# Attention with a fused projection: moving the row maxima of two query tiles within a slot

## The chip, the cores and the metric

One Trainium2 chip, one core. The time is device microseconds for one execution of the whole kernel, the median of several runs. Smaller is better.

## The reference

Sixteen images of 512 channels and 32 x 32 = 1024 positions go through an attention layer with 8 heads of 64 channels, an output projection with bias, a normalisation by the mean square over channels and a residual:

```python
qkv = jnp.einsum('bchw,oc->bohw', x, w_qkv)
q, k, v = jnp.split(qkv, 3, axis=1)
q = q.reshape(b, HEADS, HEAD_DIM, n) * SCALE        # HEAD_DIM 64, SCALE 64 ** -0.5
sim = jnp.einsum('bhdi,bhdj->bhij', q, k)
attn = jax.nn.softmax(sim, axis=-1)
out = jnp.einsum('bhij,bhdj->bhid', attn, v)
y = jnp.einsum('bchw,oc->bohw', out, w_out) + b_out[None, :, None, None]
mean_sq = jnp.mean(y * y, axis=1, keepdims=True)
y = y * jax.lax.rsqrt(mean_sq + SCALE) * rms_scale[None, :, None, None]
return y + x
```

## The kernel before

**Tiling.** A batch (image) is worked off in 8 slots; a slot is one pair of heads (slot // 2) and one half of 512 query positions (slot % 2). Within a slot there are 8 steps, one for each tile of 128 keys, and 16 places, t = 0 to 15. At every even place t TensorE computes the scores of step t / 2 for the two heads of the pair (`scores`, lines 707 and 716: two products per head, since every operand is kept as a high and a low part). ScalarE turns them into `probs` (L816), GpSimd adds the probs up in `prob_sum` (L1211, L1207), and TensorE multiplies them with the values (`values`, L729) into `pv`. The values of steps 0 to 3 of a slot run at place 9 of it, those of steps 4 to 7 at place 1 of the next slot, followed by `sums` (L648), which adds the partitions of `prob_sum`.

**What fills the odd places.** The work for later slots is put at odd places by `items_at`, which lists items and the PSUM bank of each (0 to 3 of the tile `aux`). Q, K0, K1 and V0 to V3 are projections (L549 for Q and K, L587 for V); O0 and O1 are the output projection (L616), R the mean of squares, T the transposed maxima (L601). The items M0 to M3 (called M00, M01 and so on, the second digit being the head) are products of one tile of 128 queries with all keys of the next slot; VectorE takes their row maxima (L1040), which stand in for the softmax maximum. One head's product fills two banks: M00 takes banks 0 and 1, M01 banks 2 and 3. In M1 and M3 the first head is counted in two pieces, M10 in bank 0 and N10 in bank 1: VectorE reduces bank 0 first (L1046), which frees it, then the rest (L1052); M11 is in banks 2 and 3. The maxima's matmuls have line 673 for tile 0 and line 692 for the others.

**What sets the order.** Every engine runs a program written out by hand, in order. An item that writes a bank first waits in `claim` until all earlier items in that bank have been read (`aux_free`); with `two=True` it waits for the bank beside it as well. VectorE handles at each place first the items of `items_at` in their order (maxima, k_l of the K items at L1033, and so on), then the reciprocals of the softmax sums (`invert_sums`, L1098, two halves, at INVERT_SUMS_AT), then `normalise` (L1105, at NORMALISE_AT), then its share of the normalisation of y (`invert`, L1092; `scale_y`, L1111, at SCALE_AT). ScalarE copies K to `k_hh` (L848), V to `v_sb` (L858), the sums to `inv_sum` (L879), and makes `o_hi` (L885, at OUTPUT_HIGH_AT); GpSimd makes `o_lo` (L357) in front of the addition of step 4 and adds the residual (`add_resid`, L1233) at the steps of RESIDUAL_AT in slots 1 and 2. The output product O0 stands at place 11 and needs `o_lo`.

Before, at place 1, TensorE runs: values of steps 4 and 5; M0; values of steps 6 and 7; sums; M1. At place 9 it runs the values of steps 0 to 3, M2 in front of the value number VALUES_FIRST[slot], and M3 at the end. Place 3 has K0 in slots 0, 2 and 4, a V item in slots 1, 3, 6 and 7, and nothing in slot 5; places 5 and 7 have the two halves of K1 in slots 0, 2 and 4, V items in others.

Of the kernel before, what the change touches and what calls it, by code (L numbers as in the profile page):

```python
# [17 lines left out]

SLOTS, STEPS, TILES = 8, 8, 4
PLACES = 2 * STEPS
SLOT_QUERIES = 2
RING = 6


INVERT_SUMS_AT = ((2, 2),) * 8
NORMALISE_AT = (2,) * 8
OUTPUT_HIGH_AT = (4, 8, 4, 4, 4, 6, 4, 4)
OUTPUT_LOW_AT = 4  # L30

REPEAT_K_AT = (8, 9)
# [2 lines left out]
SPLIT_MAXIMA = (1, 3)  # L35


VALUES_FIRST = (2, 1, 2, 1, 2, 1, 2, 1)


TURN_OF_MAXIMA = 7
# [12 lines left out]
SCALE_BY_GPSIMD = ((0,), (0, 1))  # L54
SCALE_BY_ACT_AT = ((0, 8), (1, 8))
SCALE_AT = ({1: (1, 1), 2: (1, 3), 3: (1, 4)}, {2: (2, 4), 3: (2, 10)})
RESIDUAL_AT = ((0, 1, 4, 4), (0, 1, 4, 5))


SPLIT_HIGH_AT = ((5, 0),) * 4 + ((6, 0),) * 4  # L60
# [11 lines left out]
def items_at(slot, t, first, last):  # L72

    following = not (last and slot == SLOTS - 1)
    projected = not (last and slot >= SLOTS - SLOT_QUERIES)
    preceding = not (first and slot == 0)
    out = []
    if t in (1, 9) and following:
        for it in (0, 1) if t == 1 else (2, 3):
            out.append((f"M{it}0", 0))  # L80
            if it in SPLIT_MAXIMA:
                out.append((f"N{it}0", 1))
            out.append((f"M{it}1", 2))
    if t == 3 and slot in (0, 2, 4):
        out.append(("K0", 0))
    elif t == 3 and (slot in (1, 3) or slot == 6 and projected or slot == 7 and following):
        out.append(({1: "V0", 3: "V2", 6: "V1", 7: "V2"}[slot], 0))
    if t == 5 and slot == 6 and projected:
        out.append(("K0", 1))
    if t == 7:  # L90
        if slot in (0, 2, 4):
            out.append(("K1", 1))
        elif slot in (1, 3):
            out.append((f"V{slot}", 1))
        elif slot == 5 and not last:
            out.append(("V0", 1))
        elif slot == 6 and projected:
            out.append(("K1", 2))
        elif slot == 7 and following:
            out.append(("V3", 1))  # L100
    if (slot, t) in MEAN_AT and not first:
        out.append(("R", 2))
    if t == (11 if following else LAST_OUTPUT_AT) and preceding:
        out.append(("O0", 0))
    if t == (13 if following else LAST_OUTPUT_AT) and preceding:
        out.append(("O1", 2))
    if t == 15:
        if following:
            out.append(("T", 2))
        if projected:  # L110
            out.append(("Q", 0))
    return out
# [33 lines left out]
def attention_kernel(nc, x, wqkv, wout, bias, scale, consts, out):  # L146
# [27 lines left out]
    with ctx:  # L174
# [330 lines left out]
        def _(pe):  # L505
            def claim(body, slot, name, two=False):

                k, n = body.at(slot, name)
                if body.plan is not pro or n > 0:
                    pe.wait_ge(aux_free[k], n)  # L510
                if two:
                    claim_beside(body, slot, name)
                return k

            def claim_beside(body, slot, name):
                other, n = beside_counts(body.plan, body.b, (slot, name))
                if body.plan is not pro and pro.end[other] or body.plan is pro and n > 0:
                    pe.wait_ge(aux_free[other], n)

            def wait_w(body, chunk, next_batch):  # L520
# [32 lines left out]
            def item(body, slot, name, turn=None, part=None):  # L553
# [19 lines left out]
                elif name[0] == "V":  # L573
                    chunk = VA if slot >= 5 else VB
                    if body.plan is not pro:
                        k = body.at(slot, name)[0] if part == 1 else claim(body, slot, name)
                    wait_w(body, chunk, slot >= 5)
                    w = w_ring[:, RING_OF[chunk]]
                    for i in range(2) if part is None else (part,):
                        jt = 2 * int(name[1]) + i  # L580
                        n = 0
# [152 lines left out]
            def one(body):  # L734
                for slot in range(SLOTS):
                    if body.first and slot == 0:
                        pe.wait_ge(q_repeated, 2)
                        pe.wait_ge(k_repeated, 4)
                    before = (body, SLOTS - 1, True) if slot == 0 else (body, slot - 1, False)
                    preceding = not (body.first and slot == 0)  # L740
                    for t in range(PLACES):
                        names = [name for name, _ in items_at(slot, t, body.first, body.last)]
                        if t % 2 == 0:
                            scores(body, slot, t // 2)
                        elif t == 1:
                            if preceding:
                                values(before[0], before[1], 4, before[2])
                                values(before[0], before[1], 5, before[2])
                            if "M00" in names:
                                maxima_of_tile(body, slot, 0)  # L750
                            if preceding:
                                values(before[0], before[1], 6, before[2])
                                values(before[0], before[1], 7, before[2])
                                sums(body, slot)
                            if "M10" in names:
                                maxima_of_tile(body, slot, 1)
                        elif t == 9:
                            for j in range(STEPS // 2):
                                if j == VALUES_FIRST[slot] and "M20" in names:
                                    maxima_of_tile(body, slot, 2)  # L760
                                if j == 2 and "O0" in names:
                                    item(body, slot, "O0")
                                    item(body, slot, "O1")
                                values(body, slot, j, False)
                            if "M30" in names:
                                maxima_of_tile(body, slot, 3)
                        else:
                            if t == 5:
                                for name, _ in items_at(slot, 7, body.first, body.last):
                                    if in_halves(slot, name):  # L770
                                        item(body, slot, name, part=0)
                            if t == 13 and body.last and slot == SLOTS - 1:
                                values(body, slot, 4, False)
                                values(body, slot, 5, False)
                                item(Body(epi, B - 1, False, True), 0, "R0")
                            for name in names:
                                if t == 7 and in_halves(slot, name):
                                    item(body, slot, name, part=1)
                                elif name == "Q":
                                    item(body, slot, "Q", (body, slot))  # L780
                                elif name != "T" or "Q" not in names:
                                    item(body, slot, name)
# [542 lines left out]
```

## Time and profile before

| | us |
|---|---|
| median of 3 runs | 3956.9 |
| lowest and highest | 3954.56, 3996.69 |
| the profiled execution's own time | 3978.09 |
| its span, first to last instruction | 3976.0 |
| TensorE busy | 3911.9 (98%) |
| VectorE busy | 2803.0 (70%) |
| ScalarE busy | 2313.7 (58%) |
| GpSimd busy | 2966.9 (75%) |
| mean granted TensorE clock | 0.994 of full speed |

Busy time is the time in which an engine had an instruction in work. For TensorE the ends of matmuls are modelled and neighbouring matmuls overlap, so distances between starts say more than durations. A row that groups several instructions gives the start of the first, the time that they covered, and their number.

### The profile page before, as it was taken

The page shows a single profiled execution, that of the slowest core. Times are in us where ns is not written, and L with a number is a line of the kernel's source. Part 1 is how long each engine was busy: PE and PEld are TensorE (multiplying, and loading weights), DVE is VectorE, ACT ScalarE, POOL GpSimd, SP SyncE. Part 2 cuts the span into 40 slices and gives each one's busy share as a digit, 9 for nine tenths or more (in the row PEclk, how much of TensorE's full clock was granted, in tenths as well). Part 3 has the DMA queues.
Part 4 walks back from the last instruction along what each step waited for, and adds up shares of the span by engine and source line. Part 5 has one row for each costly group of instructions (what it writes and reads, how often), then busy time and mean ns, then how long its engine had stood idle before and what let it go on. Part 6 is the DMA issues. An engine that isn't in the chain of part 4 may idle for free.

```text
span 3976.0 us, 53150 instructions
## 1 busy us (share of the span) xinstructions
PE 3911.9 (98%) x18630; PEld 2460.2 (62%) x18630; DVE 2803.0 (70%) x2899; ACT 2313.7 (58%) x4048; POOL 2966.9 (75%) x2332
## 2 busy tenths in 40 slices
PE   8999999999999999999999999999999999999997
PEld 5666666656666666665666666666665666666663
DVE  6667676676766767677686776767667676676775
ACT  4556565555655656565565665655556556565654
POOL 5678777776877778777787777877777777787776
PEclk9999999999999999999999999999999999999998
DMA  3111111111111201102011020111111111111100
GB/s 149 49 47 54 43 67 51 43 54 43 67 51 43 74 22 70 58 33 75 27 67 56 35 72 32 64 54 38 69 54 43 54 38 69 54 51 45 63 33 22
DMA packets 71847, 212.18 MB, mean 53 GB/s; under 512 B 8216, under 2 KB 9368, under 8 KB 58784
## 3 DMA queue, kind: packets, MB, share of 16 engines
q1 hardware_dynamic: 71584, 208.80, 14.7%
q8 instruction: 150, 2.46, 0.3%
q14 instruction: 113, 0.93, 0.1%
HBM read 168.92 MB, written 39.85 MB: 53 GB/s over the span
## 4 chain that ended last, share of the span: by engine, by line
PE 96%; DVE 1%; issue 1%; ACT 0%; DMA 0%; POOL 0%; SPq 0%; ACTq 0%; DVEq 0%; POOLq 0%
PE pv L729 24%; PE aux L549 17%; PE score L707 13%; PE score L716 12%; PE aux L587 9%; PE aux L616 9%; PE aux L692 7%; PE pv L648 3%; PE aux L673 2%; ACT probs L816 0%; DVE inv_sum L1098 0%; DVE k_l L1033 0%; PE aux L601 0%; DVE maxima L1040 0%; PE aux L626 0%
## 5 line engine op out<-in xcount | busy, mean ns | idle before, releaser
L1211 POOL TENSOR_TENSOR prob_sum<-prob_sum,probs 128x512 f32<-128x512 f32 x1536 | 1964.6, 1308 | 356.6 <-ACT probs L816 356.6
L816 ACT ACTIVATE probs<-score 128x512 f32<-128x512 f32 x2048 | 1111.0, 595 | 783.8 <-PE score L716 777.3
L1040 DVE TENSOR_REDUCE maxima<-aux 128x1 fp32r<-128x1024 f32 x768 | 914.0, 1218 | 416.1 <-PE aux L692 269.8
L729 PE MATMUL pv<-probs,v_sb 128*64 128x512 f32 x4096 | 998.1, 608 | 0.0
L707 PE MATMUL score<-q_hl,k_hh 128*128 128x512 f32 x2048 | 841.8, 411 | 9.1 <-ACT probs L816 9.1
L716 PE MATMUL score<-q_hm,k_l 72*128 72x512 f32 x2048 | 814.7, 398 | 0.5 <-DVE q_hm L1058 0.5
L549 PE MATMUL aux<-x_hi,w_ring 128*128 128x512 f32 x2048 | 654.6, 397 | 10.2 <-DMA scale_sb<-scale 9.3
L1207 POOL TENSOR_TENSOR prob_sum<-probs 128x512 f32<-128x512 f32 x256 | 325.1, 1292 | 393.7 <-ACT probs L816 391.6
L729 PEld LDWEIGHTS pv<-probs,v_sb 128*64 128x64 f32 x4096 | 249.6, 136 | 483.4 <-issue 475.6
L707 PEld LDWEIGHTS score<-q_hl,k_hh 128*128 128x128 f32 x2048 | 387.5, 189 | 179.4 <-issue 87.0
L549 PEld LDWEIGHTS aux<-x_hi,w_ring 128*128 128x128 f32 x2048 | 387.3, 189 | 97.6 <-DMA scale_sb<-scale 9.3
L1098 DVE RECIPROCAL inv_sum<-inv_sum 128x256 f32<-128x256 f32 x254 | 427.0, 1723 | 8.6 <-ACT inv_sum L879 5.7
L716 PEld LDWEIGHTS score<-q_hm,k_l 72*128 72x128 f32 x2048 | 388.3, 190 | 69.1 <-DVE q_hm L1058 1.1
L549 PE MATMUL aux<-x_lo,w_ring 128*128 128x512 f32 x1024 | 401.3, 392 | 0.0
L587 PE MATMUL aux<-w_ring,x_hi 128*128 128x256 f32 x1984 | 363.1, 282 | 0.0
L692 PEld LDWEIGHTS aux<-k_hh,q_hm 64*128 64x128 f32 x762 | 117.8, 186 | 345.9 <-issue 268.2
L587 PEld LDWEIGHTS aux<-w_ring,x_hi 128*128 128x128 f32 x1984 | 320.6, 191 | 17.3
L1058 DVE TENSOR_TENSOR q_hm<-aux,tile_mask 8x512 fp32r<-8x512 f32 x256 | 163.7, 676 | 223.2 <-PE aux L601 223.2
L1046 DVE TENSOR_REDUCE aux<-aux 128x1 f32<-128x513 f32 x256 | 179.3, 700 | 192.4 <-PE aux L692 189.6
L692 PE MATMUL aux<-k_hh,q_hm 64*128 64x512 f32 x762 | 291.8, 455 | 19.8 <-DVE k_l L1033 17.8
L1074 DVE TENSOR_TENSOR y_sb<-y_sb,aux 128x1024 f32<-128x1024 f32 x192 | 232.7, 1212 | 111.0 <-PE aux L616 110.3
L692 PE MATMUL aux<-k_hh,q_hl 64*128 64x512 f32 x762 | 291.9, 456 | 0.0
(114 smaller groups left out, 5123.6 us busy)
## 6 DMA issues: line engine op xcount, KB each, us to landing
w_ring<-w_split SPq DMA_DIRECT2D x93, 1024.0 KB, 4.8
stage<-x SPq DMA_DIRECT2D x252, 256.0 KB, 4.6
out<-stage SPq DMA_DIRECT2D x124, 256.0 KB, 2.0
w_split<-w_ring SPq DMA_DIRECT2D x3, 1024.0 KB, 12.3
w_split<-y_sb SPq DMA_DIRECT2D x3, 1024.0 KB, 3.8
y_sb<-wqkv SPq DMA_DIRECT2D x4, 512.0 KB, 8.5
probs<-wqkv SPq DMA_DIRECT2D x2, 512.0 KB, 7.2
probs<-wout SPq DMA_DIRECT2D x1, 1024.0 KB, 8.2
```

Source lines behind the costliest of these rows:

```text
L549: last = pe.matmul(out_ap, w[:, wp, k, cols], xp[:, k, xcols], start=(k == 0 and n == 0), stop=(k == KT - 1 and n == 2))
L587: last = pe.matmul(to[:, i * WCOLS:(i + 1) * WCOLS], xp[:, c, jt * P:(jt + 1) * P], w[:, wp, c, :], start=(n == 0), stop=(n == 3 * KT - 1))
L616: last = pe.matmul(bank(k + i), w[:, pair, m * P:(m + 1) * P], o[:], start=(n == 0), stop=(n == 2))
L692: last = pe.matmul(bank(k + h), q_hi_at(nhalf, e, h, it), k_hh[rows, npair % 2, e, h * HALF:(h + 1) * HALF], start=True, stop=True)
L707: pe.matmul(score[e][:], k_hh[:, pair % 2, e, keys], q_hl[:, half, e, :], start=True, stop=False)
L716: pe.matmul(score[e][:], k_l1[0:D + 2 * IT, pair % 2, e, keys], q_hm[0:D + 2 * IT, half, e, :], start=False, stop=True).then_inc(score_rea ...
L729: pe.matmul(pv[half][e * D:(e + 1) * D, :], v_sb[:, pair // 2, j, (pair % 2) * P + e * D:(pair % 2) * P + (e + 1) * D], probs[:, (b * SLOT ...
L816: act.activation(probs[:, step % RING, e, :], score[e][:], ACT.Exp, scale=SOFT).then_inc(prob_ready, 1)
L1040: dve.tensor_reduce(maxima[:, n:n + 1], bank(k, 2), AX_X, ALU.max).then_inc(aux_free[k], 1)
L1098: dve.reciprocal(inv_sum[:, cols], inv_sum[:, cols]).then_inc(inv_ready, 1)
L1207: pool.tensor_tensor(prob_sum[:, e, :], probs[:, (step - 1) % RING, e, :], probs[:, step % RING, e, :], ALU.add).then_inc(prob_added, 1)
L1211: pool.tensor_tensor(prob_sum[:, e, :], prob_sum[:, e, :], probs[:, step % RING, e, :], ALU.add).then_inc(prob_added, 1)
```

## The change

At place 1 TensorE computes all four values and the sums, then M0. M1 moves to place 3, behind the scores of step 1 and in front of the projection of that place; VectorE's list moves with it, since both go by `items_at`. VectorE inverts the sums and normalises the output at place 4 in place of 2, and ScalarE makes `o_hi` at place 8 in every slot. In slots 3 and 7 M2 stands in front of all values of place 9 (VALUES_FIRST 1 becomes 0), and the V item of place 7 goes to bank 3 in place of bank 1, with a claim on bank 2 too. The residual adds of the second half, in slot 2, move from steps 4 and 5 to 2 and 4. The banks of the maxima stay as they are.

```diff
-INVERT_SUMS_AT = ((2, 2),) * 8
-NORMALISE_AT = (2,) * 8
-OUTPUT_HIGH_AT = (4, 8, 4, 4, 4, 6, 4, 4)
+INVERT_SUMS_AT = ((4, 4),) * 8
+NORMALISE_AT = (4,) * 8
+OUTPUT_HIGH_AT = (8,) * 8
...
-VALUES_FIRST = (2, 1, 2, 1, 2, 1, 2, 1)
+VALUES_FIRST = (2, 1, 2, 0, 2, 1, 2, 0)
...
-RESIDUAL_AT = ((0, 1, 4, 4), (0, 1, 4, 5))
+RESIDUAL_AT = ((0, 1, 4, 4), (0, 1, 2, 4))
...
-    if t in (1, 9) and following:
-        for it in (0, 1) if t == 1 else (2, 3):
+    if t in (1, 3, 9) and following:
+        for it in {1: (0,), 3: (1,), 9: (2, 3)}[t]:
...
         elif slot in (1, 3):
-            out.append((f"V{slot}", 1))
+            out.append((f"V{slot}", 1 if slot == 1 else 3))
...
         elif slot == 7 and following:
-            out.append(("V3", 1))
+            out.append(("V3", 3))
...
-                        k = body.at(slot, name)[0] if part == 1 else claim(body, slot, name)
+                        k, _ = body.at(slot, name)
+                        if part != 1:
+
+                            claim(body, slot, name, two=k == 3)
...
                                 values(before[0], before[1], 5, before[2])
-                            if "M00" in names:
-                                maxima_of_tile(body, slot, 0)
-                            if preceding:
                                 values(before[0], before[1], 6, before[2])
                                 values(before[0], before[1], 7, before[2])
                                 sums(body, slot)
-                            if "M10" in names:
-                                maxima_of_tile(body, slot, 1)
+                            if "M00" in names:
+                                maxima_of_tile(body, slot, 0)
...
                         else:
+                            if "M10" in names:
+                                maxima_of_tile(body, slot, 1)
...
-                            for name in names:
+                            for name in [name for name in names if name[0] not in "MN"]:
```

## Rows read from the trace of the kernel before

**Rows 1.** The page: busy time by engine (its share of the span); the chain.

```profile
PE 3911.9 (98%) x18630; PEld 2460.2 (62%) x18630; DVE 2803.0 (70%) x2899; ACT 2313.7 (58%) x4048; POOL 2966.9 (75%) x2332
...
PE 96%; DVE 1%; issue 1%; ACT 0%; DMA 0%; POOL 0%; SPq 0%; ACTq 0%; DVEq 0%; POOLq 0%
```

**Rows 2.** Waits of TensorE: line, what it waited for, us in total, times, longest.

```profile
PE aux L692 <- DVE k_l L1033: 17.8, 3, 6.0
```

**Rows 3.** Timeline of TensorE, slot 2 into 3: start, us, what, number.

```profile
2061.53 0.40 PE L707 MATMUL score<-q_hl,k_hh 128*128 128x512 f32 x1
2061.77 0.39 PE L716 MATMUL score<-q_hm,k_l 72*128 72x512 f32 x1
2062.09 1.94 PE L729 MATMUL pv<-probs,v_sb 128*64 128x512 f32 x8
2063.96 0.49 PE L673 MATMUL aux<-k_hh,q_hm 64*128 64x512 f32 x1
...
2064.62 1.94 PE L729 MATMUL pv<-probs,v_sb 128*64 128x512 f32 x8
2066.38 1.03 PE L648 MATMUL pv<-prob_sum,ones_d 128*64 128x512 f32 x4
2067.34 0.49 PE L692 MATMUL aux<-k_hh,q_hm 64*128 64x512 f32 x1
...
2068.00 0.50 PE L707 MATMUL score<-q_hl,k_hh 128*128 128x512 f32 x1
2068.34 0.40 PE L716 MATMUL score<-q_hm,k_l 72*128 72x512 f32 x1
...
2069.05 0.62 PE L549 MATMUL aux<-x_hi,w_ring 128*128 128x512 f32 x2
...
2094.19 0.50 PE L673 MATMUL aux<-k_hh,q_hm 64*128 64x512 f32 x1
...
2096.62 1.03 PE L648 MATMUL pv<-prob_sum,ones_d 128*64 128x512 f32 x4
```

**Rows 4.** Timeline of VectorE: one row of slot 1, then slot 2.

```profile
2039.67 0.78 DVE L1111 SCALAR_TENSOR_TENSOR y_sb<-y_sb,scale_sb,rms_a 128x512 f32<-128x512 f32 x1
...
2064.72 2.36 DVE L1040 TENSOR_REDUCE maxima<-aux 128x1 fp32r<-128x1024 f32 x2 [0.39 <-PE aux L673]
2067.91 0.70 DVE L1046 TENSOR_REDUCE aux<-aux 128x1 f32<-128x513 f32 x1 [0.83 <-PE aux L692]
...
2069.25 1.21 DVE L1040 TENSOR_REDUCE maxima<-aux 128x1 fp32r<-128x1024 f32 x1
2070.38 3.35 DVE L1098 RECIPROCAL inv_sum<-inv_sum 128x256 f32<-128x256 f32 x2
2073.77 0.69 DVE L1105 TENSOR_TENSOR o_norm<-inv_sum,pv 128x512 f32<-128x512 f32 x1
...
2075.79 1.84 DVE L1111 SCALAR_TENSOR_TENSOR y_sb<-y_sb,scale_sb,rms_a 128x512 f32<-128x512 f32 x1
2077.66 1.39 DVE L1033 TENSOR_TENSOR k_l<-aux,k_hh 64x512 fp32r<-64x512 f32 x2
2079.87 2.36 DVE L1040 TENSOR_REDUCE maxima<-aux 128x1 fp32r<-128x1024 f32 x2 [0.82 <-PE aux L692]
```

**Rows 5.** Timeline of TensorE at place 9 of slot 2: M2.

```profile
2079.33 0.50 PE L692 MATMUL aux<-k_hh,q_hm 64*128 64x512 f32 x1
```

**Rows 6.** Timeline of TensorE's weight loads there: M3's second head.

```profile
2082.28 0.18 PEld L692 LDWEIGHTS aux<-k_hh,q_hm 64*128 64x128 f32 x1 [0.24 <-DVE maxima L1040]
```

**Rows 7.** Timeline of ScalarE, slot 2: copies of K0.

```profile
2071.98 1.21 ACT L848 ACTIVATE k_hh<-aux 64x512 fp32r<-64x512 f32 x2 [2.11 <-PE aux L549]
```

**Rows 8.** Timeline of VectorE and TensorE, slot 2 of the fourth batch.

```profile
843.81 7.97 DVE L1111 SCALAR_TENSOR_TENSOR y_sb<-y_sb,scale_sb,rms_a 128x512 f32<-128x512 f32 x1
...
853.35 0.76 PE L692 MATMUL aux<-k_hh,q_hm 64*128 64x512 f32 x1 [5.95 <-DVE k_l L1033]
```

**Rows 9.** Windows there: length, busy by engine (number), granted clock, DMA share, GB/s.

```profile
853.00:860.00 7.00, 6.65 (x20) 2.61 (x21) 3.57 (x5) 0.18 (x1) 0.12 (x1) 0.59 0.10 37
```

**Rows 10.** Timeline of GpSimd, the end of slot 2.

```profile
2089.12 5.02 POOL L1211 TENSOR_TENSOR prob_sum<-prob_sum,probs 128x512 f32<-128x512 f32 x4
```

More of the change, by code:

```diff
@@ L516, in claim_beside @@
                 other, n = beside_counts(body.plan, body.b, (slot, name))
-                if body.plan is not pro and pro.end[other] or body.plan is pro and n > 0:
+                if n > 0:
                     pe.wait_ge(aux_free[other], n)
```

## The prediction

> **What bounds the kernel.** I read the page first: TensorE is busy for 98% of the span, and the chain that ended last is TensorE for 96% [rows 1]. VectorE (70%) and GpSimd (75%) have room on average. So the time is the length of TensorE's stream, and an edit counts by what it adds to that stream: slower switching between kinds of matmul, or a wait. The waits say that there is hardly one: the largest entry is 17.8 us in three pieces [rows 2]. All three are one event: a VectorE scaling that took 7.97 us where its neighbour takes 1.84, after which TensorE stood 5.95 us [rows 8], and the granted clock of the next 7 us was 0.59, that is, a mixture of 2.4 and 1.2 GHz [rows 9]. One such event costs 5.95 + 0.41 x 7 = 8.8 us at most, three about 26 us. The profiled execution took 3978.1 us; without them it would be near 3952, next to the 3954.6 to 3956.9 of two of the three unprofiled runs. So I add my sum to the median, 3956.9 (on the profiled execution's own time it is the same sum on 3978.1).
>
> Next, the timeline of TensorE at place 1 of one slot [rows 3], slot 2, which stands for all 128. Its order is: values of steps 4 and 5 (1.87 us), M0 (0.66), values of 6 and 7 (1.76), sums (0.96), M1 (0.66), then the scores of step 1 (1.05), then the projection. The reader should see that nothing waits. Then VectorE over the same slot [rows 4]: it starts on M0 0.76 us after M0's first matmul and needs 2.36 us for its two reductions. They end at 2067.08, and M1, which writes the same banks, starts at 2067.34. M0's reductions are hidden under values and sums, with 0.26 us to spare. That cover is what the change takes away.
>
> **Moving M0 behind the sums and M1 behind the scores of step 1.** Let T be the start of M0. Before, M1 came at T + 3.38. Now only the scores of step 1 lie between: M0 0.66, scores 1.05, and a score-to-maxima switch that the trace of before does not have. Its bounds are 0 and 0.10 us, the latter the step from score to values (0.32 us from the last score matmul to the first value, where a score follows a score in 0.23 [rows 3]); I take 0.10. So M1 is next on TensorE at T + 1.8.
> The banks are not free then. M10 takes banks 0 and 1, which M00 held: its reduction ends at T + 0.76 + 1.23 = T + 2.0. M11 takes banks 2 and 3, which M01 held: T + 0.76 + 2.36 = T + 3.12. With 0.05 us for the semaphore M11 starts at T + 3.17. The 0.05 and the wait itself can be seen at place 9: M2 starts at 2079.33, its reductions end at 2079.87 + 2.36 = 2082.23, and the weights of M3's second head are loaded at 2082.28 [rows 5, 6]. There M3 comes 2.53 us behind M2 and still waits a little; M1 would now come 1.8 us behind M0.
> Then the projection (K0, V0, V2 or V1, by slot) claims bank 0, which M10 has to leave. VectorE can start M10's 0.70 us reduction only when both of M0's are done, so bank 0 is free at T + 3.12 + 0.70 + 0.05 = T + 3.87. Without waits the projection would start at T + 1.8 + 0.66 = T + 2.45. That is 1.42 us in the seven slots with a projection at place 3. Slot 5 has none: the scores follow M11 at T + 3.17 + 0.42 = T + 3.6 instead of T + 2.45, which is 1.15 us. Per batch: 7 x 1.42 + 1.15 = 11.1 us. TensorE's stream has no slack elsewhere to take this back.
>
> **Slot 1** has a scaling on VectorE at place 1, behind M0 and M1 before, and now between them, since M1 is at place 3. It took 0.78 us in this place [rows 4] and 1.84 in slot 2; I take 1.2. The projection's bank is freed that much later: + 1.2.
>
> **K1 in front of M2.** M2 also claims bank 1 (or 0), where K1 lies until VectorE has written k_l. The events of [rows 8] show how tight that is in slot 2: a scaling that took 6.13 us longer stopped TensorE for 5.95, so about 0.2 us is spare. VectorE's work after the change, in slot 2: M1's reductions take 2.56 us (2067.91 to 2070.46), T + 3.12 to 5.7. K0 stands before the reciprocals in program order now: its last matmul is at T + 3.87 + 2.7, ScalarE's copies start 0.2 later and take 0.6 each [rows 7], so VectorE idles to T + 7.5 and has k_l at T + 8.9. Then the reciprocals 3.35, o_norm 0.69, scaling 1.84 and k_l of K1 1.39 [rows 4]: T + 16.15. M2 was at T + 15.37 (2079.33 - 2063.96); it is now at 15.37 - 2.57 + 1.42 + 0.04 = T + 14.26. So slot 2 waits 1.9 us more. In slot 4, without the scaling, it is 0.1; in slot 0, with the mean's 0.69 on VectorE and 0.46 on TensorE, 0.35. Sum 2.35 per batch. The norm of the output, moved from place 2 to 4, costs nothing by itself: o_norm is ready near T + 13 and the output product stands at place 11, past M2 and M3.
>
> **Small items.** A stretch of column-tiled matmuls costs 0.11 us where it ends (1.87 against 1.76 for the same eight [rows 3]) and about 0.05 where it starts. Place 1 loses one such stretch (-0.15) and gains the switch to maxima after scores and from maxima to the projection (0.10 each, the latter as 2068.00 to 2068.34 against 0.23): + 0.04 per slot, 0.35 per batch. VALUES_FIRST 1 to 0 in slots 3 and 7 takes away one stretch in each: -0.3. V3 in bank 3 is nothing: ScalarE copies it in 0.6 us under the scores, 0.93.
> The Trainium skill, TensorEngine Tiling (Array Packing), Key Properties, says that changing the tiling mode drains the engine. By that rule alone place 1 has five changes before (full, column, row, column, row, full) and five after, so the sum would have 0 in place of the 0.35; the rows price the changes unequally. The forecast does not turn on it.
>
> **Residual adds, slot 2.** GpSimd's adds move to steps 2 and 4, but VectorE scales these rows at places 4 and 10. In program order GpSimd now waits for the scaling that ends at T + 14.75, and for the one at place 10, near T + 23.5; with the rest of its list (one add, six sums of 1.26) it ends near T + 32.4. The next slot's sums come at T + 30.2 + 3.4 - 0.95 = T + 32.6 (30.2 is from M0 to M0, 2063.96 to 2094.19 [rows 3]; 3.4 is 1.42 + 1.9 and the small items, rounded). Before, GpSimd was done at 2094.14 and the sums stood at 2096.6: 2.5 us spare [rows 10], and now about nothing. I take 0; up to 2 us per batch for the range.
>
> **Sum.** 11.1 + 1.2 + 2.35 + 0.05 = 14.7 us in each of 14 middle batches = 206. The first batch lacks the scalings and means: 11.3. The last has no projection in slots 6 and 7 and no maxima in slot 7: 13. Together 230 us: 3956.9 + 230 = 4187.
>
> **Rivals.** (A) Forecast: the direct wait and the K1 waits, 4150 to 4225. Chance 0.62.
> (B) The direct wait alone. For: VectorE's order leaves room, if K0's copies come sooner than I think. 11.1 x 16 = 178, at 4135; without the wait for bank 0 too, 1.15 x 8 x 16 = 147, at 4104. Chance 0.15.
> (C) The waits feed on each other: GpSimd's sums late by 2 us in slot 3, and 0.7 us more at K1 in three slots: + 4 per batch, 4187 + 65 = 4250. For: no spare in [rows 10]. Against: the stretched slot gives GpSimd time too. Chance 0.14.
> (D) The clock falls at these waits. After a wait of 5.95 us it fell, to a mean of 0.59 over 7 us [rows 8, 9]. Against: the new waits are 0.3 to 1.9 us with matmuls between. If each of 128 slots paid the 0.41 x 7 = 2.9 us of that event, 4187 + 370 = 4557. Chance 0.03.
> (E) The other side: no wait at M1. The one mechanism is that M0's banks are free when M1 arrives; the price is 0 if the two reductions end before T + 1.8, in 1.0 us instead of 2.36. Then only the small items remain, 16 x 0.05 = 1 us: 3958. Against: [rows 4] and the wait in [rows 6]. Chance 0.05 for this, with anything within 1%. An actual gain has only the lost stretches, 0.15 us x 160 = 24 us, 0.6%: 0.01 for more than 1%.
>
> **Numbers.** Predicted 4187. About 1% is what a measurement of this kernel can tell from no change. The range takes A whole, most of B down to 4110 and C to 4255; outside are the rest of B and C, D and E, some 0.17. Faster by over 1%: 0.01. Within 1%: 0.05. Slower by over 1%: 0.94.
>
> **What would show it.** TensorE's waits should hold a line of maxima matmuls at L692 waiting for VectorE's maxima at L1040, some 127 times and about 1.2 us each in all, and the projection waiting for L1046 about 0.7 us, 111 times. TensorE's busy share should fall from 98% to about 94%. The distance from one slot's sums to the next should grow from 30.2 by 1.4 in slots 3, 6, 7 and by 3 or more in slot 2, and M2 there should wait for k_l (L1033). If M1's first matmul stands at T + 1.8 with its second head right behind, the step on the banks is wrong. If slots 0, 2 and 4 grow like slot 3, it is the K1 step; if slot 3's sums wait for prob_sum, it is (C).

## The result and the profile after

The changed kernel takes 4199.5 us (median of 4 runs, 4191.8 to 4204.8) where the kernel before takes 3957.3: 1.061 times as long, with a 95% interval of 1.058 to 1.064. The profiled execution took 4195.8 us with a span of 4193.7. (The diff above leaves out one changed line, L517: the claim on a neighbouring bank now waits whenever that bank has earlier items. A run below that has this line too takes as long as the kernel before.)

In the page of the changed kernel, TensorE is busy for 3 points less of the span, and the chain, which was 96% TensorE [rows 1], now runs through VectorE for 17%:

```profile
PE 3995.8 (95%) x18630; PEld 2520.2 (60%) x18630; DVE 2767.7 (66%) x2899; ACT 2309.4 (55%) x4048; POOL 2948.7 (70%) x2332
...
PE 80%; DVE 17%; issue 2%; ACT 1%; DMA 0%; POOL 0%; SPq 0%; DVEq 0%; POOLq 0%
```

TensorE's busy time itself rose by 84 us with the same 18630 matmuls. Only part of that is slower matmuls: the run below with one scaling moved has the waits of this kernel, less time at half clock than the kernel before (42.8 us against 47.6), and still 54 us more busy time (3965.8). My reading, which no run shows, is that matmuls with waits between them overlap less, so that their modelled durations cover more time. The waits of TensorE in the changed kernel (us in total, times, longest) answer to [rows 2]; L696 are the maxima of tiles 1 to 3, L1043 and L1049 the reductions, L1036 the k_l:

```profile
PE aux L696 <- DVE maxima L1043: 102.7, 254, 0.5
PE aux L696 <- DVE k_l L1036: 25.3, 47, 0.9
PE aux L591 <- DVE aux L1049: 23.6, 15, 1.6
```

The timeline of TensorE at places 1 to 3 of slot 2 after the change, against [rows 3]. The time ahead of a row's name is its start and how long the group lasted; a wait stands in brackets:

```profile
2175.54 3.65 PE L733 MATMUL pv<-probs,v_sb 128*64 128x512 f32 x16
2179.03 1.03 PE L652 MATMUL pv<-prob_sum,ones_d 128*64 128x512 f32 x4
2179.99 0.50 PE L677 MATMUL aux<-k_hh,q_hm 64*128 64x512 f32 x1
...
2180.65 0.50 PE L711 MATMUL score<-q_hl,k_hh 128*128 128x512 f32 x1
...
2181.46 0.39 PE L720 MATMUL score<-q_hm,k_l 72*128 72x512 f32 x1
2182.12 0.47 PE L696 MATMUL aux<-k_hh,q_hm 64*128 64x512 f32 x1 [0.28 <-DVE maxima L1043]
...
2183.16 0.49 PE L696 MATMUL aux<-k_hh,q_hm 64*128 64x512 f32 x1 [0.54 <-DVE maxima L1043]
...
2183.77 0.73 PE L550 MATMUL aux<-x_hi,w_ring 128*128 128x512 f32 x2
```

With T = 2179.99, M1's heads start at T + 2.13 and T + 3.17, and the projection at T + 3.78. The bracketed waits are only the part in which the modelled matmuls had all ended; the distances between starts give the whole cost. VectorE in the same slot, against [rows 4]:

```profile
2180.75 2.36 DVE L1043 TENSOR_REDUCE maxima<-aux 128x1 fp32r<-128x1024 f32 x2 [2.96 <-PE aux L677]
2183.02 0.69 DVE L1049 TENSOR_REDUCE aux<-aux 128x1 f32<-128x513 f32 x1
...
2184.36 1.22 DVE L1043 TENSOR_REDUCE maxima<-aux 128x1 fp32r<-128x1024 f32 x1
2187.52 1.39 DVE L1036 TENSOR_TENSOR k_l<-aux,k_hh 64x512 fp32r<-64x512 f32 x2 [1.95 <-ACT k_hh L851]
2188.94 3.37 DVE L1101 RECIPROCAL inv_sum<-inv_sum 128x256 f32<-128x256 f32 x2
2192.34 0.69 DVE L1108 TENSOR_TENSOR o_norm<-inv_sum,pv 128x512 f32<-128x512 f32 x1
2192.95 0.75 DVE L1114 SCALAR_TENSOR_TENSOR y_sb<-y_sb,scale_sb,rms_a 128x512 f32<-128x512 f32 x1
2193.61 1.38 DVE L1036 TENSOR_TENSOR k_l<-aux,k_hh 64x512 fp32r<-64x512 f32 x2
2195.67 2.35 DVE L1043 TENSOR_REDUCE maxima<-aux 128x1 fp32r<-128x1024 f32 x2 [0.68 <-PE aux L696]
```

VectorE starts on M0 0.76 us after its first matmul, as before, but works through M0 while TensorE stands in front of M1. From M1 on it waits 1.95 us for K0's copies, which now come before the reciprocals.

The distance from one slot's sums to the next slot's, in us (each the median over batches 0 to 14, from the starts of the sums' matmuls in the two timelines, and likewise for the experiments below), names where it went:

```
from the sums of slot   1      2      3      4      5      6      7      0     sum
before                30.71  30.27  30.26  30.18  27.87  33.07  30.26  30.63  243.2
changed               35.04  32.53  31.48  31.87  28.62  34.45  31.48  32.61  258.1
growth                 4.33   2.26   1.22   1.69   0.75   1.38   1.22   1.98   14.9
```

In slot 1 the clock takes part. The waits there, with the scaling that VectorE does between M0 and M1:

```profile
2148.12 0.49 PE L696 MATMUL aux<-k_hh,q_hm 64*128 64x512 f32 x1 [0.54 <-DVE maxima L1043]
...
2150.20 0.50 PE L591 MATMUL aux<-w_ring,x_hi 128*128 128x256 f32 x2 [1.57 <-DVE aux L1049]
```

```profile
2147.99 1.54 DVE L1114 SCALAR_TENSOR_TENSOR y_sb<-y_sb,scale_sb,rms_a 128x512 f32<-128x512 f32 x1
2149.45 0.69 DVE L1049 TENSOR_REDUCE aux<-aux 128x1 f32<-128x513 f32 x1
```

And the windows over it (length, busy by engine with the number of instructions, then the granted clock, the DMA share and GB/s):

```profile
2144.00:2148.00 4.00, 3.30 (x16) 1.32 (x12) 2.29 (x3) 3.94 (x6) 2.83 (x3) 1.00 0.00 0
2148.00:2152.00 4.00, 2.31 (x15) 1.99 (x16) 3.96 (x6) 1.77 (x4) 4.00 (x4) 0.93 0.20 70
2152.00:2155.00 3.00, 3.00 (x15) 2.96 (x15) 3.00 (x2) 0.23 (x1) 2.82 (x2) 0.53 0.00 0
2155.00:2159.00 4.00, 4.00 (x29) 3.68 (x28) 3.96 (x4) 2.51 (x5) 2.99 (x3) 1.00 0.17 66
```

TensorE did 2.31 us of work in 4 us, and then ran near half of full speed, that is at 1.2 GHz, for 3.4 us. The record of the granted clock has 26 stretches at half clock, 119.5 us in all; the kernel before has 7 with 47.6 us, three of them behind long scalings as in [rows 8]. In the two middle batches without a stretch in slot 1 that slot took 33.54 us.

Of the 26 stretches 13 fall in slot 1, 4 at the start and the end of the kernel, and 9 in slots 2, 3 and 6. Each of these 9 starts 4.8 to 4.9 us behind the sums of its slot, right behind the two short waits of M1, and the slot has no longer wait in front of it. This is slot 3 of the eleventh batch, TensorE's rows and the windows:

```profile
2733.36 0.46 PE L696 MATMUL aux<-k_hh,q_hm 64*128 64x512 f32 x1 [0.26 <-DVE maxima L1043]
...
2734.39 0.50 PE L696 MATMUL aux<-k_hh,q_hm 64*128 64x512 f32 x1 [0.54 <-DVE maxima L1043]
...
2735.00 0.74 PE L591 MATMUL aux<-w_ring,x_hi 128*128 128x256 f32 x2
```

```profile
2731.00:2735.00 4.00, 3.10 (x14) 1.38 (x12) 2.98 (x4) 1.68 (x3) 1.67 (x2) 1.00 0.00 0
2735.00:2738.50 3.50, 3.50 (x16) 3.50 (x17) 3.47 (x3) 0.00 (x0) 0.83 (x1) 0.51 0.00 0
```

Slot 3 of the batch before it has the same waits and 3.08 us of work in the same 4 us, and its clock stayed at full speed. A stretch of 3.4 us makes slot 3 longer by 1.49 us (32.97 against 31.48).

### The profile page after: what moved, and what is told of

Read it like the earlier page. It is cut to its first block, busy times and chain, and to the rows that moved or that the text cites. A ratio compares the mean times of both kernels' runs of the same rounds, so it can differ in the third digit from the quotient of the medians.

```text
span 4193.7 us, 53644 instructions
## 1 busy us (share of the span) xinstructions
PE 3995.8 (95%) x18630; PEld 2520.2 (60%) x18630; DVE 2767.7 (66%) x2899; ACT 2309.4 (55%) x4048; POOL 2948.7 (70%) x2332
## 4 chain that ended last, share of the span: by engine, by line
PE 80%; DVE 17%; issue 2%; ACT 1%; DMA 0%; POOL 0%; SPq 0%; DVEq 0%; POOLq 0%
PE pv L733 20%; PE aux L550 14%; PE aux L591 10%; PE score L711 9%; PE aux L620 8%; PE score L720 8%; DVE maxima L1043 7%; PE aux L696 5%; DVE inv_sum L1101 4%; DVE k_l L1036 3%; PE pv L652 3%; PE aux L677 2%; DVE aux L1049 2%; DVE y_sb L1114 1%; ACT k_hh L851 1%
## 5 line engine op out<-in xcount | busy, mean ns | idle before, releaser
L1214 POOL TENSOR_TENSOR prob_sum<-prob_sum,probs 128x512 f32<-128x512 f32 x1536 | 1940.5, 1294 | 471.0 <-ACT probs L819 470.9
L1043 DVE TENSOR_REDUCE maxima<-aux 128x1 fp32r<-128x1024 f32 x768 | 914.3, 1218 | 683.2 <-PE aux L677 471.0
L733 PE MATMUL pv<-probs,v_sb 128*64 128x512 f32 x4096 | 958.1, 602 | 0.0
L550 PE MATMUL aux<-x_hi,w_ring 128*128 128x512 f32 x2048 | 663.8, 402 | 14.9 <-DMA scale_sb<-scale 9.0
L733 PEld LDWEIGHTS pv<-probs,v_sb 128*64 128x64 f32 x4096 | 262.6, 136 | 511.3 <-issue 462.3
L696 PE MATMUL aux<-k_hh,q_hm 64*128 64x512 f32 x762 | 319.3, 466 | 128.0 <-DVE maxima L1043 102.7
L591 PE MATMUL aux<-w_ring,x_hi 128*128 128x256 f32 x1984 | 402.2, 302 | 28.5 <-DVE aux L1049 23.6
L696 PEld LDWEIGHTS aux<-k_hh,q_hm 64*128 64x128 f32 x762 | 126.9, 184 | 429.7 <-issue 253.8
L591 PEld LDWEIGHTS aux<-w_ring,x_hi 128*128 128x128 f32 x1984 | 342.8, 207 | 60.1 <-DVE aux L1049 48.1
L696 PE MATMUL aux<-k_hh,q_hl 64*128 64x512 f32 x762 | 324.4, 472 | 0.0
L851 ACT ACTIVATE k_hh<-aux 64x512 fp32r<-64x512 f32 x256 | 151.8, 593 | 291.6 <-PE aux L550 288.4
```

What stands on the lines that cost most here:

```text
L550: last = pe.matmul(out_ap, w[:, wp, k, cols], xp[:, k, xcols], start=(k == 0 and n == 0), stop=(k == KT - 1 and n == 2))
L591: last = pe.matmul(to[:, i * WCOLS:(i + 1) * WCOLS], xp[:, c, jt * P:(jt + 1) * P], w[:, wp, c, :], start=(n == 0), stop=(n == 3 * KT - 1))
L696: last = pe.matmul(bank(k + h), q_hi_at(nhalf, e, h, it), k_hh[rows, npair % 2, e, h * HALF:(h + 1) * HALF], start=True, stop=True)
L733: pe.matmul(pv[half][e * D:(e + 1) * D, :], v_sb[:, pair // 2, j, (pair % 2) * P + e * D:(pair % 2) * P + (e + 1) * D], probs[:, (b * SLOT ...
L1043: dve.tensor_reduce(maxima[:, n:n + 1], bank(k, 2), AX_X, ALU.max).then_inc(aux_free[k], 1)
L1214: pool.tensor_tensor(prob_sum[:, e, :], prob_sum[:, e, :], probs[:, step % RING, e, :], ALU.add).then_inc(prob_added, 1)
```

## The experiments

Each run was made beside runs of the kernel before on the same chip, whose median lies between 3956 and 3972 us by chip; so ratios are compared, and slot lengths. A time in us set against an expected one can be off by up to these 15 us. Where only one time was taken, no ratio is given.

### M0's reductions made short

```diff
-dve.tensor_reduce(maxima[:, n:n + 1], bank(k, 2), AX_X, ALU.max)
+src = bank(k)[:, 0:64] if name[1] == "0" else bank(k, 2)
+dve.tensor_reduce(maxima[:, n:n + 1], src, AX_X, ALU.max)
```

> The changed kernel, but VectorE's two reductions of M0 read 64 of the 1024 columns, so part of the row maximum is left out; matmuls, banks and waits are the same. Theory (M1 and the projection wait for banks that M0's reductions hold, 2.36 us): the reductions shrink to some 0.4 us together, M1 starts at T + 1.8 without a wait, and slots 1, 3, 5, 6, 7 go back to the length of before. What stays is the K1 wait, since VectorE's list from K0 on is as long as it was: 1 to 2 us in slot 2, 0.2 to 0.4 in slots 0 and 4. 3957 + 16 x 1.5 to 2.5 = 3980 to 4000. Rival (the switches between kinds of matmul, or the scores and projection following each other less well, cost the time): this edit touches no matmul, so the time stays near 4200.

Measured: 4064.8 us, ratio 1.023 (1.021 to 1.026). Most of the loss goes with this edit, which touches no matmul, so the banks held by M0 are shown as a cause. But the number was missed by 65 to 85 us (50 to 70 by the ratio), and slots 3 and 7 did not go back: 30.86 and 30.87 us against 30.26. The waits say why:

```profile
PE aux L591 <- DVE aux L1050: 48.4, 62, 1.4
PE aux L550 <- DVE aux L1050: 29.0, 49, 0.9
PE aux L696 <- DVE k_l L1036: 25.4, 47, 0.9
```

M1's wait for M0 is gone. The projection waits instead for M10's own reduction (here L1050), since it follows M1 directly; before, the scores of step 1 lay between the two and hid it. The bank 0 wait thus has two parts, of which M0's reductions are only one.

### M0's and M10's reductions made short

```diff
+start = k * HALF if name[1] != "1" else first - 63
-dve.tensor_reduce(aux[:, first:first + 1], aux[:, k * HALF:first + 1], AX_X, ALU.max
+dve.tensor_reduce(aux[:, first:first + 1], aux[:, start:first + 1], AX_X, ALU.max
```

> The kernel with M0's short reductions (64 of 1024 columns), and M10's reduction, which frees bank 0, shortened too (64 columns of 513); part of the row maxima of tiles 0 and 1 is left out. With M0's reductions short alone the time came to 1.023 times that of before, and every slot with a projection at place 3 still waited 0.6 us for M10's own reduction: the scores of step 1 used to stand between M1 and the projection and no longer do. Theory: with both short that wait goes; slots 3 and 7 grow by 0.1 us or less over before, slots 0, 2 and 4 keep the K1 wait (0.4 to 1.1 us each): 2 to 3 us per batch, 1.01 times before. Rival (the switches are dearer than 0.1 us): slots 3 and 7 keep 0.3 us or more, and the time stays above 1.017.

Measured: 4003.0 us, ratio 1.011 (1.010 to 1.013), as expected. Slots 3 and 7 are at 30.40, 0.14 us above before, a little more than expected and less than the rival's 0.3; the 0.11 to 0.15 that M2's place gives back in these two slots (a run below) is in it. The switches can be read here without a wait:

```profile
2113.02 0.40 PE L720 MATMUL score<-q_hm,k_l 72*128 72x512 f32 x1
2113.35 0.50 PE L696 MATMUL aux<-k_hh,q_hm 64*128 64x512 f32 x1
...
2114.21 0.50 PE L591 MATMUL aux<-w_ring,x_hi 128*128 128x256 f32 x2
```

From the last score to M1 it is 0.33 us, 0.10 above the 0.23 between scores: the value that the prediction took. From M1 to the projection it is 0.86 us, of which 0.66 are M1; the 0.2 are left of the wait for M10 (its reduction, started at 2113.92, took 0.23, and the projection came 0.06 later). What stays of the loss is mostly slots 1, 2, 4 and 0 (1.02, 1.16, 0.56 and 0.84 us). Slot 5 is 0.44 us shorter than before.

### The scaling of slot 1 put behind M1

```diff
-SCALE_AT = ({1: (1, 1), 2: (1, 3), 3: (1, 4)}, {2: (2, 4), 3: (2, 10)})
+SCALE_AT = ({1: (1, 3), 2: (1, 3), 3: (1, 4)}, {2: (2, 4), 3: (2, 10)})
```

> The changed kernel with one scaling of slot 1 on VectorE (m = 1, place 1) moved behind M1's reductions (place 3). In the changed kernel slot 1 grew by 4.3 us, of which 1.4 is the wait of every slot, about 1.4 the scaling between M0 and M1, and the rest a stretch of 3.4 us at half clock that follows in nearly every batch. Theory: without the scaling in between, slot 1 grows by about 1.4 only, and the half-clock stretches in slot 1 vanish with it: 15 x 2.9 = 43 us less, 4155. Rival (the clock stretches come from the many short waits in the kernel as a whole, not from the long one of slot 1): only 15 x 1.4 = 21 us less, 4178, and the stretches stay.

Measured: 4151.8 us, ratio 1.045 (1.042 to 1.048), 4155 expected. The profiled spans (4149.9 and 4193.7) differ by 44 us, 43 expected; by the ratios it is 62, as the kernel before took 3971 on this chip. Slot 1 fell from 35.04 to 32.91 us. That is 2.2 above before and not 1.4, as M2 in this slot now waits for VectorE, whose list the moved scaling made later:

```profile
PE aux L696 <- DVE rms_a L1088: 8.0, 14, 0.6
```

Of the 26 half-clock stretches 6 are left, at the start and the end and two in the second batch's first slots. The direct waits are as they were (102.4 us in 253 pieces for L696 on L1043). So the longer wait of slot 1 is what drops the clock there, and the rival is refuted for slot 1. But it is not the only thing that can: in the changed kernel 9 stretches, and in this run two, followed nothing but the short waits of 0.3 and 0.5 us inside 2.4 us. Most slots have these waits and no stretch. Why the 9 went with the long wait of another slot is open.

### The norm back at place 2, between M0 and M1 on VectorE

```diff
-INVERT_SUMS_AT = ((4, 4),) * 8
-NORMALISE_AT = (4,) * 8
+INVERT_SUMS_AT = ((2, 2),) * 8
+NORMALISE_AT = (2,) * 8
```

> The changed kernel with the reciprocals of the sums and the normalisation of the output back at place 2, so that VectorE does them between M0 and M1. Theory (the projection waits for M10's reduction, which stands in VectorE's list behind all that is in front of it): the reciprocals and o_norm, 4.05 us, move in front of M10's reduction; the projection starts 4.05 us later in seven slots, and slot 5's scores do not wait for M10. 7 x 4.05 = 28 us per batch, less what the K1 wait gives back (about 1): 4200 + 15.5 x 27 = 4620, and more where the clock falls. Rival (M1 waits only for M0's banks, the projection for something else): M1's wait is unchanged and the time stays within 1% of 4200.

Measured once: 4889.6 us. The waits:

```profile
PE aux L591 <- DVE aux L1049: 282.5, 62, 5.6
PE aux L550 <- DVE aux L1049: 197.8, 48, 4.2
PE aux L696 <- DVE maxima L1043: 102.9, 254, 0.5
```

M1's own wait is the same as in the changed kernel, and the projection's has grown to some 4.4 us (480.3 us in 110 pieces): the order on VectorE decides, as the theory has it. The size was missed by 270 us, for two reasons. Slot 5 was expected to stay and grew by 5.6 us: it has no projection at place 3, but its V item at place 5 needs the other bank, which N10 holds until VectorE is through the same work:

```profile
PE aux L591 <- DVE maxima L1055: 57.3, 15, 3.8
```

That is some 85 us over the kernel. The rest goes with the clock: the record has 128 stretches, 925 us, nearly one in each slot. Slot 3 grew by 6.1 us over the changed kernel, 4.05 of them the reciprocals and o_norm; the other 2.0 fall to a stretch of 6.8 us at half clock, in part of which TensorE had work.

### M1 right behind M0

```diff
-                            if "M00" in names:
-                                maxima_of_tile(body, slot, 0)
+                            if "M00" in names:
+                                maxima_of_tile(body, slot, 0)
+                                maxima_of_tile(body, slot, 1)
```

(and the M1 items back at place 1 in the list)

> The changed kernel with M1 right behind M0 at place 1, in front of the scores of step 1. Theory by the banks: M1's second head still starts at T + 3.17, but nothing covers it; scores of step 1 then end at T + 3.6 + 1.0, so the projection at T + 4.6 finds bank 0 free. Against the kernel before (M1 without a wait at T + 0.66) that is 3.6 - 1.32 = 2.3 us per slot, 18.3 per batch, plus the K1 waits of 1 to 2: near 3957 + 16 x 19.5 = 4270. Rival (the place behind the scores is what costs, by switches): M1 back at place 1 brings the time back towards 3957.

Measured once: 4411.8 us, above the 4270 expected and far from the rival's 3957. M1's place behind the scores is not what costs. The record has 90 stretches at half clock, 419 us in all, and the slots without one separate the two causes: there slots 1, 3, 6 and 7 grew by 2.20, 2.00, 2.12 and 1.97 us over before, where the theory has 2.3, and slots 2, 4 and 0, with the K1 wait, by 2.35, 2.44 and 2.72. Slot 5 had a stretch in every batch; with one of 3.4 us it grew by 3.3. So the banks give the sign and, at 2.0 to 2.2 us per slot, nearly all of the size expected of them. From these slots I estimate 4230 without a stretch (17.6 us per batch); the rest goes with the clock, at 1.4 to 2.8 us more in a slot that has one.

### The norm alone moved, in the kernel before

```diff
-INVERT_SUMS_AT = ((2, 2),) * 8
-NORMALISE_AT = (2,) * 8
-OUTPUT_HIGH_AT = (4, 8, 4, 4, 4, 6, 4, 4)
+INVERT_SUMS_AT = ((4, 4),) * 8
+NORMALISE_AT = (4,) * 8
+OUTPUT_HIGH_AT = (8,) * 8
```

> The kernel before with only the norm of the output later: reciprocals and o_norm at place 4, o_hi at place 8 in every slot. Theory (these places cost nothing in themselves): VectorE's list between M1 and M2 has the same work in another order; K0's copies come before the reciprocals, so VectorE idles about 1 us for them in slots 0, 2 and 4, and slot 2 had only 0.3 us spare in front of M2: up to 0.7 us in slot 2, at most 15 us in all, ratio 1.000 to 1.004. Rival (the later o_hi and o_lo hold up the output product or the probabilities): growth in all slots, 1.01 or more.

Measured: 3979.4 us, ratio 1.005 (1.004 to 1.007), a little above the range. Slots 2, 4 and 0 grew by 0.88, 0.35 and 0.62 us (31.15, 30.53, 31.25), all others by nothing. The wait is that of the changed kernel (25.3 us in 47 pieces) to 0.3 us:

```profile
PE aux L692 <- DVE k_l L1033: 25.6, 47, 0.9
```

The wait for K1's k_l thus comes with the norm's move alone, and M1's move adds nothing to it. The later o_hi and o_lo cost nothing: a growth in slots 1, 3, 5, 6 or 7 would have shown it.

### The reciprocals of slots 0, 2 and 4 made short

```diff
+if slot in (0, 2, 4):
+    cols = slice(part * HALF // 2, part * HALF // 2 + 64)
 dve.reciprocal(inv_sum[:, cols], inv_sum[:, cols]).then_inc(inv_ready, 1)
```

> The changed kernel with the reciprocals of the sums in slots 0, 2 and 4 over 64 columns in place of 256 in each half; the rest of the columns stays a plain sum, so part of the division is left out. VectorE has some 2.4 us less between K0 and K1 in these slots. Theory (M2 waits for K1's k_l, which stands behind the reciprocals that the change put behind K0; moving the norm alone in the kernel before gave 0.88, 0.35 and 0.62 us in slots 2, 4 and 0): the same three slots lose these 0.9, 0.35 and 0.6 us here, 15.5 x 1.85 = 28 us less, 4170 where the changed kernel has 4200. Rival (the growth of these slots beyond that of slot 3 comes from the claim of the projection, since K0 is read by VectorE and V by ScalarE): the lengths of slots 0, 2 and 4 stay.

Measured: 4172.5 us, ratio 1.054 (1.051 to 1.056) where the changed kernel has 1.061. Slots 2, 4 and 0 lost 0.94, 0.29 and 0.59 us, and the wait of M2 for k_l is gone. The two causes add up.

### The residual adds of slot 2 late again

```diff
-RESIDUAL_AT = ((0, 1, 4, 4), (0, 1, 2, 4))
+RESIDUAL_AT = ((0, 1, 4, 4), (0, 1, 4, 5))
```

> The changed kernel with the residual adds of slot 2 back at steps 4 and 5. In the changed kernel GpSimd stood idle for the scaling at place 4, and the scaling took 0.75 us instead of 1.84, so that K1's k_l was ready 1.1 us sooner than forecast. Theory (the scaling is slow when GpSimd works beside it): with the adds late GpSimd is busy during it, the scaling takes 1.8 us again, and slot 2 grows from 32.5 to 33.6: 15 x 1.1 = 16 us more, 4216. Rival (the scaling's time does not depend on GpSimd): the time stays at 4200 or falls.

Measured: 4187.2 us, ratio 1.058 (1.057 to 1.059). Slot 2 grew, from 32.53 to 33.19 us, and the scaling in front of K1's k_l took 1.38 us in place of 0.75:

```profile
2184.81 1.38 DVE L1114 SCALAR_TENSOR_TENSOR y_sb<-y_sb,scale_sb,rms_a 128x512 f32<-128x512 f32 x1
```

That is 0.66 us per batch, against 1.1 expected. So this scaling does depend on GpSimd, which is idle beside it in the changed kernel and was adding here. But GpSimd at work is not enough to make it slow. In the run with the norm alone moved the adds were late too, GpSimd was busy through the same scaling, and it took 0.74 to 0.75 us in all 15 batches; there GpSimd's four additions beside it took 5.47 us, where four took 5.02 in [rows 10]:

```profile
2079.77 0.74 DVE L1111 SCALAR_TENSOR_TENSOR y_sb<-y_sb,scale_sb,rms_a 128x512 f32<-128x512 f32 x1
```

```profile
2076.17 5.47 POOL L1211 TENSOR_TENSOR prob_sum<-prob_sum,probs 128x512 f32<-128x512 f32 x4
```

The kernel as a whole came out 12 us below the changed kernel, not above it, though the intervals of the two ratios overlap a little. This run has 15 half-clock stretches and 77 us in place of 26 and 120: 11 in slot 1 for 13, 4 at the start and the end in both, and none for the 9 elsewhere. An estimate of half the time at half clock, 21 us less, with 0.66 x 15 = 10 us more gives about the 12. Why fewer slots drop is open; slot 1 has the same waits in both.

### Two attempts at a faster kernel

Both start from the kernel before. The first:

```diff
-VALUES_FIRST = (2, 1, 2, 1, 2, 1, 2, 1)
+VALUES_FIRST = (2, 1, 2, 0, 2, 0, 2, 0)
```

with the V items of slots 3, 5 and 7 in bank 3.

> The kernel before with M2 in front of all values of place 9 in slots 3, 5 and 7 (VALUES_FIRST 0) and the V item of place 7 in bank 3 there. Theory (a stretch of column-tiled matmuls costs 0.15 us beyond its matmuls): each of these slots loses one, 3 x 0.15 = 0.45 us per batch, 7 us in all, ratio 0.998. Rival (M2's second head then waits for the copy of V in bank 3): these slots get longer.

Measured: 3955.1 us, ratio 0.9994 (0.9985 to 1.0002), no difference. Slots 3 and 7 became shorter by 0.15 and 0.11 us as expected, slot 5 longer by 0.16; the waits of TensorE have no line for it, so why is open.

The second added K1 in bank 2 in slots 0 and 4, M2 one value sooner in slots 0, 4 and 6, and M1 at place 3 in slot 5, where M2 went back to its old place.

> The kernel before with what the runs showed to be of use. M2 in front of all values in slots 3 and 7 (V item in bank 3): 0.13 us less in each. K1 in bank 2 in slots 0 and 4, and M2 in front of the second value in slots 0, 4 and 6, so that M3 comes 3.4 us behind M2 instead of 2.5 and no longer waits for its bank: 0.1 to 0.2 us less in each, if K1's k_l is ready in time. In slot 5 alone, which has no projection at place 3 so that the scores of step 2 waited for ScalarE, M1 behind the scores of step 1, with the norm at place 4: up to 0.45 us less. But M0 stays in front of the values of steps 6 and 7. Sum 1.0 to 1.2 us per batch, 17 us in all, ratio 0.996. If M2 comes too early for K1, slots 0, 4 and 6 grow instead, by up to 0.3 us each.

Measured: 4047.3 us, ratio 1.022 (1.019 to 1.024): a miss.

```profile
PE aux L550 <- DVE rms_a L1090: 50.0, 15, 3.3
```

In slot 0, K1 in bank 2 stands behind the mean R, which holds that bank until VectorE is through the reciprocals and K0: 5.1 us more, of which 3.3 are the wait; in 12 of the batches the clock fell in this slot, too. M1 at place 3 in slot 5 cost 0.68 us. Without these two:

> The version before without the two edits that lost: slot 0 keeps K1 in bank 1 and M2 in front of the third value (with K1 in bank 2 it waited up to 3.3 us for the mean R, which holds that bank until VectorE is through the reciprocals), and slot 5 keeps M1 and the norm as in the kernel before (M1 behind the scores cost 0.68 us there, not a gain). What is left is what gained in that version: slots 3 and 7 (M2 first) 0.15 and 0.12, slot 4 (K1 in bank 2, M2 one value sooner) 0.09, slot 6 (M2 one value sooner) 0.12 us. 0.5 us per batch, 8 us in all, ratio 0.998, at the edge of what can be measured.

Measured: 3964.3 us beside 3971.5 for the kernel before on the same chip, ratio 0.997 (0.994 to 1.001). The slots add up to 242.8 us for 243.2. A gain of 0.2 to 0.3% is what both numbers suggest, and the interval reaches past 1: it is not established.

## Why the prediction was right, and where it was wrong

Forecast 4187 in a range of 4110 to 4255; measured 4199.5. Term by term, per middle batch:

**The direct wait: 11.1 us forecast.** The positions came out as worked out: M1's heads at T + 2.13 and T + 3.17 (T + 2.0 and T + 3.17 forecast), the projection at T + 3.78 (3.87). Slots 3 and 7 grew by 1.22 with 0.15 of gain from M2's place, so 1.37 for 1.42 + 0.04. Slot 5 grew by 0.75, not 1.15 + 0.04. The step that failed there is "TensorE's stream has no slack elsewhere": slot 5 has nothing at place 3, so the scores of step 2 followed those of step 1 and waited for ScalarE, and M1 now stands in that gap (the run with both reductions short has slot 5 0.44 us below before). In the trace of before, slot 5, the last score of step 1 starts at 2159.50 and the first of step 2 0.61 us later, where scores follow each other in 0.24:

```profile
2160.11 0.50 PE L707 MATMUL score<-q_hl,k_hh 128*128 128x512 f32 x1 [0.21 <-ACT probs L816]
```

In the other slots the term was right in size, for a reason that I had split wrongly: even with free banks 0.6 us of it would stay for M10's own reduction, since the scores that covered it moved away. The expectation for the first experiment missed by that.

**Slot 1: 1.2 forecast.** The scaling took 1.54 us, and without a clock stretch slot 1 grew by 33.54 - 30.71 = 2.83, for 1.42 + 1.2 + 0.04 = 2.66.

**K1 in front of M2: 2.35 forecast, 1.85 measured** (0.88, 0.35 and 0.62 in slots 2, 4 and 0 with the norm alone moved, for 1.9, 0.1 and 0.35; short reciprocals took 0.94, 0.29 and 0.59 out of the changed kernel). In slot 2 the scaling was taken at the 1.84 us of [rows 4], and it took 0.75 with GpSimd idle, which stood waiting for just this result. (It took 0.75 beside a busy GpSimd, too, in the run with the norm alone moved.) And the sentence "the norm of the output, moved from place 2 to 4, costs nothing by itself" is wrong: moved alone it makes all of this wait, because VectorE then idles for K0's copies before it takes up the reciprocals. The mechanism was named, but put down to M1.

**The clock: left out of the sum.** I gave 0.03 to a fall of the clock in all slots and did not think of one slot. It fell above all where the waits are longest, in slot 1, and 9 times in slots 2, 3 and 6: the middle batches took 259.1 us on average, and 243.2 + 13.3 without a stretch (slots as in the batch with the least, 256.5). That is 2.6 us per batch, 36 us over 14. The terms of the sum, against it, came out 1.4 us per batch too high, most of it in slots 2 and 5. These errors went against each other.

**GpSimd and the next sums: 0 forecast.** TensorE waited 0.9 us once for prob_sum, as before; the stretched slot gave GpSimd the time. Its waits for the scalings are there (46.7 us in 30 pieces), and TensorE's wait for prob_sum is no longer than before. Of the rivals, (B) is refuted by the runs on the norm, (C) by this, and (E) by the timeline. (D) was priced for every slot and came in one slot of eight, for the most part.

**The sum.** 13.3 x 14 + 2.6 x 14 = 223; the first batch grew by 11.3 (11.3 forecast), the last by some 8 (13). Together 242, which is the measured difference. The forecast had 230. That it lies only 12 us off is in part luck: 36 us for the clock were missing, and 20 in the middle batches and 5 in the last were too many. The mechanism, two waits for banks and one for k_l, is what the runs show.

**The signs to look for.** The busy share came to 95% (94 forecast). The line L696 on L1043 is there with 254 pieces, twice as many as forecast and 0.4 us each, as the profile counts only the time after the modelled end of the matmuls. The wait of the projection shows in slot 1 alone (15 pieces) in that view; in the other slots it lies in the distance between starts. Slot 2 grew by 2.3 us and not by 3 or more, and M2 waits there for k_l (L1036, 47 pieces over slots 2, 4 and 0).

## What to carry to other kernels

Before moving a producer behind the work that hid its consumer, write down for each PSUM bank when it is released and who claims it next, and follow the second claim too: here the bank passed from M0 to M1 to a projection, and the change took away the cover of both hand-overs. A wait on the bounding engine should be priced twice, once as the wait and once as what the clock does after it when waits come close together. And a reordering on an engine with 30% of idle time is free only if the new first item is ready: the norm's move cost 0.5% by making VectorE wait for an input.

## What the runs showed of the hardware

The same VectorE scaling of 128 x 512 took 0.74 to 0.75 us in all 135 places of these traces in which GpSimd was idle beside it. Beside a GpSimd at work it took from 0.74 to 1.88 us (leaving out seven of 3 or 8 us): 1.38 and 1.84 in the rows above, but 0.78 in slot 1 of the kernel before and 0.75 in slot 2 with the norm alone moved. So GpSimd's activity is needed for the slow form and does not bring it about by itself.

TensorE's granted clock fell to 1.2 GHz in or after a wait of 1.57 us that followed two shorter ones within 3.1 us, in 13 batches of the changed kernel. After the two short waits alone, 0.26 and 0.54 us, it fell in 9 slots of the changed kernel and in 12 of the run with short reciprocals, and in most slots with the same waits it did not. With a wait of 4.2 us in each slot nearly every slot had a stretch, and the time beyond the wait itself was 2 us per slot. Which slots drop differed between runs with the same waits (26 and 15 stretches); what decides it is open.

In the kernel before, three scalings of 8 us stand in the profiled execution, and two more, with waits of 5.9 us for k_l, in the first version of the second attempt; none is in the changed kernel's profile (longest 1.80 us). What they are is open.
